# A gated attention and routing block on one core: turning the softmax tile in place, two placed buffers, and a new slot table

## The chip, the cores and the metric

One core of one Trainium2 chip runs the kernel. The metric is device time in microseconds (us). The engines are TensorE (PE, its weight loads PEld), VectorE (DVE), ScalarE (ACT), GpSimd (POOL) and SyncE (SP); SP issues nearly all DMAs here.

## The reference, cut to what matters

```python
# x, ctx: (8, 512, 2048) float32; _layernorm over the last axis (2048)
x = x + tanh(g_xattn) * attn(_layernorm(x), ctx, mask, Wq.. bo)
x = x + tanh(g_ffn)   * route(_layernorm(x), router_weight, router_bias, expert_bias)

def attn(qk, v, ...):        # the 2048 columns are cut into windows of W = 128
    q, k = Wq @ qk + bq, Wk @ qk + bk        # 512 -> 256 rows = 8 heads of 32
    val  = Wv @ v + bv
    scores = einsum('bhdi,bhdj->bhij', qh, kh) / sqrt(32)     # 128 x 128 per head
    scores = where(mask > 0, scores, -1e9)
    o = einsum('bhij,bhdj->bhdi', softmax(scores), vh)
    return (Wo @ gelu(o) + bo) * mask        # 256 -> 512 rows

def route(flat, ...):        # 64 experts, the 8 largest of the softmax are kept
    w = top8(softmax(flat @ router_weight.T + router_bias))
    return flat * w.sum() + w @ expert_bias
```

## The kernel before, in words

A batch is 512 rows by 2048 columns: four tiles of 128 partitions in `X[b % 2]`. The attention works on **units** of 256 columns (two windows): 8 units a batch, 64 in all. float32 products are made of three fp32r passes (`hi*hi`, `lo*hi`, `hi*lo`), so most operands are split in a high part (ScalarE copy) and a low part (GpSimd or VectorE subtraction).

A unit `u` passes through these steps (engine, line of the profile):

- GpSimd z (L1042), ScalarE z_hi (L582), GpSimd z_lo (L1049): the normalised columns. TensorE `project` q and k (L309 to L311, 24 matmuls each), ScalarE q_full, VectorE k_full (L747).
- per window: ctx load (SP L494), ScalarE cx_hi (L598), GpSimd cx_lo (L1055), TensorE v_mm (L324 to L326, 12 matmuls), ScalarE v_full (L604).
- TensorE `scores` (L340: four mask matmuls that open four PSUM banks; L348: 32 tiled 32x128 passes), VectorE `top` (L755, four maxima), ScalarE `expo` (L614, four groups of four exponentials with their sums; L608 brings the table back), VectorE `turn_p` (L762, four transposes of 32x32 blocks), `turn_d` (L767, L771: reciprocals of the sums, spread), SP `move` (L520, 16 DMAs that carry partition quarters of T to PT), TensorE `weigh` (L365, 32 tiled 128x32 passes: the values' products), VectorE `divide` (L777).
- ScalarE `gelu` (L619 table, L622), `o_high` (L631), GpSimd `o_low` (L1066), TensorE `project_out` in two halves WO0 and WO1 (L384 to L386, 12 matmuls each), VectorE `weigh_out` (L790), GpSimd `add_x` (L1061).
- for the router: TensorE `r_turn` (hT, L403, 8 transposes), ScalarE `r_high` (L638), VectorE `r_low` (L820), TensorE `r_mm` (R, L416 and L417), VectorE `stats2` (L803).

Once a batch, after its last unit: ScalarE `c_logits` (L, L644), TensorE `c_turn` (LT, L427), VectorE `c_top` (L841 to L856), ScalarE `c_exp` (L649), VectorE `c_weights` and `c_scale`, TensorE `w_turn` (wT, L438), ScalarE `w_high` (L656), VectorE `w_low` (L883), TensorE `mix` (L453, L454, 16 pairs), ScalarE `scale_x` (L664, four, one per 128 rows), VectorE `add_mix` (x2, L894, 16), SP `store` (L530, 16), then SP `load_x` (L525, 16) of the batch two later into the same buffer, VectorE `input_stats` (bn1, L904, 16) and the norm. The first `input_stats` of each 128 rows waits for all four loads of these rows.

The order of the work on each engine is written out in advance. `SLOTS` gives each step a lag in slots; a unit starts every 16 slots, a batch every 128, a tick is an eighth of a slot. Each engine walks through the ticks and issues what is due: the slots are an order, not times, and no engine waits for a tick. `ENDS` shifts the steps of the last three units. Seven PSUM banks form a ring: `take` gives each product the bank whose planned release is earliest, and the product waits for that release's reader. `PR` is an eighth bank, for R.

In one unit the order on TensorE before is: WO1(u-3), q(u), v, hT(u-3), PV(u-2), k(u), v, WO0(u-2), S(u), R(u-3). `P` is the tile that `expo` writes and `turn_p` reads into `T[u % 2]`; there is one `PT`, so `move(u)` waits for `divide(u-1)`.

## Time and profile before

| | |
|---|---|
| median of 3 runs | 1216.48 us (1215.22 to 2746.26) |
| the profiled execution | 1222.89 us, its span 1221.1 us |
| mean granted TensorE clock | 0.988 |
| TensorE / weight loads busy | 1132.3 / 1046.8 us |
| VectorE / ScalarE / GpSimd busy | 982.0 / 1028.0 / 708.5 us |

The page splits the span by engine, follows back the chain that ended last, and groups instructions by line. A timeline row is start, duration, engine, line, operation, names, count, and in brackets the idle time before it with what ended it. Matmuls overlap, so the cost of one is the distance to the start of the next.

### The profile page before, as it was taken

The page shows a single profiled execution, that of the slowest core. Times are in us where ns is not written, and L with a number is a line of the kernel's source. Part 1 is how long each engine was busy: PE and PEld are TensorE (multiplying, and loading weights), DVE is VectorE, ACT ScalarE, POOL GpSimd, SP SyncE. Part 2 cuts the span into 40 slices and gives each one's busy share as a digit, 9 for nine tenths or more (in the row PEclk, how much of TensorE's full clock was granted, in tenths as well). Part 3 has the DMA queues.
Part 4 walks back from the last instruction along what each step waited for, and adds up shares of the span by engine and source line. Part 5 has one row for each costly group of instructions (what it writes and reads, how often), then busy time and mean ns, then how long its engine had stood idle before and what let it go on. Part 6 is the DMA issues. An engine that isn't in the chain of part 4 may idle for free.

```text
span 1221.1 us, 33356 instructions
## 1 busy us (share of the span) xinstructions
PE 1132.3 (93%) x11661; PEld 1046.8 (86%) x11661; DVE 982.0 (80%) x1921; ACT 1028.0 (84%) x3200; POOL 708.5 (58%) x660
## 2 busy tenths in 40 slices
PE   3799999999999999899999999999999989999976
PEld 3698999899979899788997999988998889979965
DVE  6658879988799877978789887988879877797757
ACT  4698998989988899888998889888998879988944
POOL 2376766467646676466764566646774657655621
PEclk9899999999999999999999999999999989999989
DMA  9377554885548754586546854477544874556433
GB/s 285 82 181 195 137 134 108 249 217 134 126 117 259 209 127 126 176 232 159 131 122 212 218 157 129 110 244 219 135 125 117 265 193 123 130 148 186 109 82 138
DMA packets 169767, 199.82 MB, mean 164 GB/s; under 512 B 27776, under 2 KB 104704, under 8 KB 169472
## 3 DMA queue, kind: packets, MB, share of 16 engines
q1 hardware_dynamic: 168736, 197.69, 59.4%
q8 instruction: 93, 1.52, 0.5%
q14 instruction: 74, 0.61, 0.2%
q10 hardware_dynamic: 864, 0.01, 0.0%
HBM read 80.06 MB, written 33.65 MB: 93 GB/s over the span
## 4 chain that ended last, share of the span: by engine, by line
PE 52%; DVE 15%; SPq 15%; issue 7%; POOL 4%; ACT 4%; DMA 3%; DVEq 0%; POOLq 0%; ACTq 0%
SPq L520 10%; PE ring L309 7%; PE ring L311 6%; PE ring L310 6%; PE ring L365 4%; DVE X L894 3%; PE ring L348 3%; PE ring L324 3%; PE ring L326 3%; PE ring L325 3%; PE ring L384 3%; PE ring L385 3%; PE ring L386 3%; PE ring L403 3%; SPq L525 2%
## 5 line engine op out<-in xcount | busy, mean ns | idle before, releaser
L614 ACT ACTIVATE P<-ring,nmx 128x128 f32<-128x128 f32 x1024 | 358.7, 402 | 55.5 <-DVE nmx L755 55.1
L309 PE MATMUL ring<-z_hi,wqk_hi 128*128 128x256 f32 x1024 | 298.6, 292 | 23.5 <-DVE z_lo L958 21.1
L311 PE MATMUL ring<-z_lo,wqk_hi 128*128 128x256 f32 x1024 | 291.4, 285 | 0.0
L310 PE MATMUL ring<-z_hi,wqk_lo 128*128 128x256 f32 x1024 | 291.3, 285 | 0.0
L614 ACT ACTIVATION_READ_ACCUMULATOR P<-ring,nmx 128x1 f32 x1024 | 248.5, 243 | 0.0
L1049 POOL TENSOR_TENSOR z_lo<-z,z_hi 128x1024 fp32r<-128x1024 f32 x62 | 147.6, 2380 | 164.5 <-ACT z_hi L582 164.5
L309 PEld LDWEIGHTS ring<-z_hi,wqk_hi 128*128 128x128 f32 x1024 | 197.3, 193 | 36.3 <-DVE wqk_lo L933 21.1
L1061 POOL TENSOR_TENSOR X<-X,xt 128x512 f32<-128x512 f32 x128 | 165.2, 1290 | 100.9 <-DVE xt L790 100.5
L762 DVE STREAM_TRANSPOSE T<-P 128x512 f32<-128x512 f32 x256 | 169.1, 690 | 42.5 <-ACT P L614 24.4
L311 PEld LDWEIGHTS ring<-z_lo,wqk_hi 128*128 128x128 f32 x1024 | 197.8, 193 | 0.0
L310 PEld LDWEIGHTS ring<-z_hi,wqk_lo 128*128 128x128 f32 x1024 | 197.7, 193 | 0.0
L1055 POOL TENSOR_TENSOR cx_lo<-cx,cx_hi 128x512 fp32r<-128x512 f32 x128 | 165.9, 1296 | 36.4 <-ACT cx_hi L598 36.4
L755 DVE TENSOR_REDUCE nmx<-ring 128x4 f32<-128x512 f32 x256 | 158.5, 681 | 16.1 <-PE ring L348 15.9
L1066 POOL TENSOR_TENSOR ot_lo<-o,ot_hi 128x512 fp32r<-128x512 f32 x63 | 81.5, 1294 | 148.4 <-ACT ot_hi L631 148.4
L384 PE MATMUL ring<-ot_hi,wo_hi 128*128 128x256 f32 x504 | 143.7, 285 | 12.2 <-POOL ot_lo L1066 12.2
L324 PE MATMUL ring<-wv_hi,cx_hi 128*128 128x256 f32 x512 | 146.6, 286 | 7.8 <-POOL cx_lo L1055 6.0
L790 DVE SCALAR_TENSOR_TENSOR xt<-ring,cst,mg 128x256 f32<-128x256 f32 x256 | 111.3, 476 | 46.1 <-PE ring L386 44.1
L325 PE MATMUL ring<-wv_lo,cx_hi 128*128 128x256 f32 x512 | 145.5, 284 | 0.0
L326 PE MATMUL ring<-wv_hi,cx_lo 128*128 128x256 f32 x512 | 145.4, 284 | 0.0
L386 PE MATMUL ring<-ot_lo,wo_hi 128*128 128x256 f32 x504 | 143.1, 284 | 0.0
L385 PE MATMUL ring<-ot_hi,wo_lo 128*128 128x256 f32 x504 | 142.8, 283 | 0.0
L1042 POOL TENSOR_SCALAR z<-X,ln 128x256 f32<-128x256 f32 x252 | 137.6, 559 | 0.7
(138 smaller groups left out, 2713.3 us busy)
## 6 DMA issues: line engine op xcount, KB each, us to landing
PT<-T SPq DMA_DIRECT2D x1024, 80.0 KB, 2.1
cx<-in_ctx SPq DMA_DIRECT2D x128, 256.0 KB, 3.7
out_y<-X SPq DMA_DIRECT2D x128, 256.0 KB, 3.1
X<-in_x SPq DMA_DIRECT2D x112, 256.0 KB, 4.2
mg<-in_mask SPq DMA_DIRECT2D x64, 128.0 KB, 3.1
X<-in_x SPq DMA_DIRECT2D x8, 512.0 KB, 7.6
sel<-rows_d SPq DMA_DIRECT2D x256, 3.0 KB
X<-in_eb SPq DMA_DIRECT2D x2, 512.0 KB, 8.5
```

The source lines that it names most:

```text
L309: e.matmul(o, wqk_hi[:, t, cols], z_hi[:, t, :], t == 0, False)
L310: e.matmul(o, wqk_lo[:, t, cols], z_hi[:, t, :], False, False)
L311: last = e.matmul(o, wqk_hi[:, t, cols], z_lo[:, t, :], False, t == DT - 1)
L324: e.matmul(o, cx_hi[:, k, :], wv_hi[:, k, :], k == 0, False)
L325: e.matmul(o, cx_hi[:, k, :], wv_lo[:, k, :], False, False)
L326: last = e.matmul(o, cx_lo[:, k, :], wv_hi[:, k, :], False, k == DT - 1)
L384: e.matmul(o, wo_hi[:, m, cols], o_hi[:, m, :], m == 0, False)
L385: e.matmul(o, wo_lo[:, m, cols], o_hi[:, m, :], False, False)
L386: last = e.matmul(o, wo_hi[:, m, cols], o_lo[:, m, :], False, m == 1)
L614: last = e.activation(P[:, n, :], bank("S", 4 * u + g)[:, k * W:(k + 1) * W], ACT.Exp, bias=nmx[u % 2][:, n:n + 1], accum_out=den[u % 2][: ...
L762: e.transpose(T[u % 2][:, :, 4 * g:4 * g + 4, :].rearrange("p b k i -> p k b i"), P[:, 4 * g:4 * g + 4, :].rearrange("p k (b j) -> p k b j ...
L1055: e.tensor_tensor(cx_lo[:], cx[p % NC][:], f32(cx_hi[:]), ALU.subtract).then_inc(cxlo_g, 1)
```

## The change: what it does, and the diff

`P` goes. `expo` writes the exponentials straight into `T[u % 2]`, in the strided layout that the transposes had as output, and `turn_p` transposes each 32x32 block where it stands. `PT` is double, each with its own semaphore. `w2` is laid over `L`. The whole slot table is new. In the new one PV(u) has lag 31.875 and S(u+2) 32, so the values' products stand directly in front of the mask rows and scores of the unit two later. In one unit the order on TensorE becomes: S(u), hT(u-3), q(u+1), WO0(u-2), v, R(u-3), k(u+1), WO1(u-2), v, PV(u-1).

```diff
 SLOTS = dict(
-    rows=-30, z32=-26.25, z_hi=-16, z_lo=-19.75, q=-14, q_ev=-6.25, k=-6.25, k_ev=-6.25,
-    c_hi=-15.5, c_lo=-13.75, v=-10.75, v_ev=-7.5, v_gap=-3.25,
-    S=-1.75, top=1, exp=4, e_gap=0.25, tp=6.25, td=7.25, mv=8.5, PV=25.25, on=23.25,
-    gelu=23, mg=2, ot_hi=24, ot_lo=27.5, WO=27.25, WO_gap=5.75, xt=29.75, x1=31, bn2=39.25,
-    hT=37.5, hT_gap=0.25, ht_hi=41.25, ht_lo=41.75, R=47.25,
-    norm2=27.5, c_base=33.5, L=36, LT=34, c_top=38.75, c_exp=37.75, c_w=40.75, c_sc=40.75, wT=43, wt_hi=43.25, wt_lo=42.25, mix=43.75, m_gap=0.25,
-    sx=44.75, sx_gap=1.25, x2=45.25, rl=48.5, rl_gap=2,
-    x_1=21, x_gap=3.5, bn1=63.25, bn1_gap=2, norm1=101.25,
+    rows=-29, z32=-28, z_hi=-24.25, z_lo=-22.25, q=-14, q_ev=-7.25, k=-6.25, k_ev=-6.5,
+    c_hi=-1, c_lo=2.5, v=6.25, v_ev=7.75, v_gap=-2.25,
+    S=0, top=0.75, exp=4, e_gap=0.25, tp=8, td=9.25, mv=12, PV=31.875, on=29.125,
+    gelu=30.625, mg=13.875, ot_hi=33.375, ot_lo=31.875, WO=36.625, WO_gap=6.75, xt=36.375, x1=39.125, bn2=51.875,
+    hT=48.625, hT_gap=0.5, ht_hi=49.875, ht_lo=49.375, R=55.125,
+    norm2=39.375, c_base=43.625, L=40.875, LT=47.875, c_top=46.875, c_exp=49.625, c_w=49.375, c_sc=49.875, wT=50.375, wt_hi=52.375, wt_lo=51.875, mix=53.375, m_gap=0.25,
+    sx=52.375, sx_gap=0.25, x2=52.375, rl=55.125, rl_gap=1.5,
+    x_1=22, x_gap=4, bn1=67.75, bn1_gap=2, norm1=99.5,
 )
 ENDS = {
...
-        P = sb("P", [128, 16, W])
-        PT = sb("PT", [128, 4, 20, 32])
+        PT = [sb(f"PT{i}", [128, 4, 20, 32]) for i in range(2)]
-        w2 = sb("w2", [128, DT, 2, NX])
+        w2 = L[:].rearrange("p (t a x) -> p t a x", t=DT, a=2)
-        pt_in = sem("pt")
+        pt_in = [sem(f"pt{i}") for i in range(2)]
...                                                     # weigh
-                e.wait_ge(pt_in, 256 * (u + 1))
+                e.wait_ge(pt_in[u % 2], 256 * (u // 2 + 1))
...                                                     # move
-                if u:
-                    e.wait_ge(on_v, u)
+                if u >= 2:
+                    e.wait_ge(on_v, u - 1)
...                                                     # expo
-                if u:
-                    e.wait_ge(tp_v, 4 * (u - 1) + g + 1)
+                if u >= 2:
+                    e.wait_ge(pt_in[u % 2], 256 * (u // 2))
-                    last = e.activation(P[:, n, :], bank("S", 4 * u + g)[:, k * W:(k + 1) * W], ACT.Exp,
-                                        bias=nmx[u % 2][:, n:n + 1], accum_out=den[u % 2][:, n:n + 1])
+                    last = e.activation(T[u % 2][:, :, n, :], bank("S", 4 * u + g)[:, k * W:(k + 1) * W].rearrange("p (b j) -> p b j", b=4),
+                                        ACT.Exp, bias=nmx[u % 2][:, n:n + 1], accum_out=den[u % 2][:, n:n + 1])
...                                                     # c_logits
                 if b:
                     e.wait_ge(lt_pe, b)
+                    e.wait_ge(wT_pe, b)
+                    e.wait_ge(ac_v, b)
...                                                     # turn_p
-                if u >= 2:
-                    e.wait_ge(pt_in, 256 * (u - 1))
                 e.wait_ge(exp_a, 4 * u + g + 1)
-                e.transpose(T[u % 2][:, :, 4 * g:4 * g + 4, :].rearrange("p b k i -> p k b i"),
-                            P[:, 4 * g:4 * g + 4, :].rearrange("p k (b j) -> p k b j", b=4)).then_inc(tp_v, 1)
+                tg = T[u % 2][:, :, 4 * g:4 * g + 4, :].rearrange("p b k i -> p k b i")
+                e.transpose(tg, tg).then_inc(tp_v, 1)
```

`turn_d`, `divide` and `c_weights` change in the same way (`pt_in[u % 2]`, `PT[u % 2]`, `w2`). `ENDS` has new values for all its entries; for the last unit: exp -0.25, tp 2.5, td 3.25, mv 30.25, PV -6.25, on -1.25, gelu 5.75, WO -6, hT 2.25, R 1.5.

## Rows read from the trace of the kernel before

**Rows 1.** The page: busy time by engine, and the last chain by engine.

```profile
PE 1132.3 (93%) x11661; PEld 1046.8 (86%) x11661; DVE 982.0 (80%) x1921; ACT 1028.0 (84%) x3200; POOL 708.5 (58%) x660
PE 52%; DVE 15%; SPq 15%; issue 7%; POOL 4%; ACT 4%; DMA 3%; DVEq 0%; POOLq 0%; ACTq 0%
```

**Rows 2.** Timeline of TensorE, around the tiled products of one unit.

```profile
575.34 1.03 PE L403 MATMUL ring<-ident,X 128*128 128x128 f32 x8
576.30 1.08 PE L365 MATMUL ring<-PT,v 128*32 128x128 f32 x32
577.32 0.39 PE L309 MATMUL ring<-z_hi,wqk_hi 128*128 128x256 f32 x1
577.54 0.28 PE L310 MATMUL ring<-z_hi,wqk_lo 128*128 128x256 f32 x1
...
583.10 0.28 PE L386 MATMUL ring<-ot_lo,wo_hi 128*128 128x256 f32 x1
583.31 0.40 PE L340 MATMUL ring<-sel,ones 32*128 32x512 bf16 x4
...
584.52 0.49 PE L416 MATMUL PR<-ht_hi,wr 128*128 128x512 f32 x1
584.86 0.40 PE L417 MATMUL PR<-ht_lo,wr 128*128 128x512 f32 x1
```

**Rows 3.** Chain of waits: PV of units 5 and 6.

```profile
142.12 1.01 PE ring L365 x32
158.03 1.01 PE ring L365 x32
```

**Rows 4.** Timeline of TensorE: PV of units 0, 3, 32, 33, 34, 61.

```profile
60.51 1.08 PE L365 MATMUL ring<-PT,v 128*32 128x128 f32 x32
...
110.21 1.08 PE L365 MATMUL ring<-PT,v 128*32 128x128 f32 x32 [1.71 <-DMA PT<-T]
...
624.35 1.08 PE L365 MATMUL ring<-PT,v 128*32 128x128 f32 x32
641.68 1.08 PE L365 MATMUL ring<-PT,v 128*32 128x128 f32 x32
669.72 1.08 PE L365 MATMUL ring<-PT,v 128*32 128x128 f32 x32
...
1154.64 1.08 PE L365 MATMUL ring<-PT,v 128*32 128x128 f32 x32
```

**Rows 5.** Waits over the whole span: waiting, for whom, us, times, longest.

```profile
DVE bnst L904 <- DMA X<-in_x: 31.8, 22, 3.9
PE ring L403 <- POOL X L1061: 15.6, 12, 3.6
```

**Rows 6.** Timelines of SP's queue and of VectorE, 977 to 991 us.

```profile
977.75 1.44 SPq L525 DMA_DIRECT2D X<-in_x  x3
...
979.77 11.27 SPq L520 DMA_DIRECT2D PT<-T  x16
...
987.48 0.69 DVE L904 BATCH_NORM_STATS2 bnst<-X 128x6 f32<-128x512 f32 x1 [3.95 <-DMA X<-in_x]
```

**Rows 7.** Timelines in the batch stage: two scalings on ScalarE, eight adds on VectorE.

```profile
652.48 4.12 ACT L664 ACTIVATE X<-X,sc 128x2048 f32<-128x2048 f32 x2
654.73 4.86 DVE L894 TENSOR_TENSOR X<-X,ring 128x512 f32<-128x512 f32 x8
```

**Rows 8.** Groups by line: the exponentials and the transposes.

```profile
L614 ACT ACTIVATE P<-ring,nmx 128x128 f32<-128x128 f32 x1024 | 358.7, 402 | 55.5 <-DVE nmx L755 55.1
L762 DVE STREAM_TRANSPOSE T<-P 128x512 f32<-128x512 f32 x256 | 169.1, 690 | 42.5 <-ACT P L614 24.4
```

**Rows 9.** Timelines at the start and end: move(0), S(63), move(63).

```profile
47.82 11.09 SPq L520 DMA_DIRECT2D PT<-T  x16
...
1161.60 0.39 PE L340 MATMUL ring<-sel,ones 32*128 32x512 bf16 x4
...
1171.91 10.00 SPq L520 DMA_DIRECT2D PT<-T  x16
```

More of the change, by code:

```diff
@@ L364, in weigh @@
                             o = bank("PV", u)[32 * g:32 * g + 32, m * U + w * W:m * U + (w + 1) * W]
-                            last = e.matmul(o, v32[p % NV][:, h * DH:(h + 1) * DH], PT[:, :, 4 * g + 2 * m + w, :], True, True)
+                            last = e.matmul(o, v32[p % NV][:, h * DH:(h + 1) * DH], PT[u % 2][:, :, 4 * g + 2 * m + w, :], True, True)
                 last.then_inc(pv_pe, 1)
@@ L515, in move @@
                 e.wait_ge(td_v, u + 1)
-                if u:
-                    e.wait_ge(on_v, u)
+                if u >= 2:
+                    e.wait_ge(on_v, u - 1)
                 for b in range(4):
                     for a in range(4):
-                        e.dma_start(PT[32 * b:32 * b + 32, a, :, :], T[u % 2][32 * a:32 * a + 32, b, :, :]).then_inc(pt_in, 16)
+                        e.dma_start(PT[u % 2][32 * b:32 * b + 32, a, :, :], T[u % 2][32 * a:32 * a + 32, b, :, :]).then_inc(pt_in[u % 2], 16)
             def load_x(b, t, c):
@@ L769, in turn_d @@
                 if u >= 2:
-                    e.wait_ge(pt_in, 256 * (u - 1))
+                    e.wait_ge(pt_in[u % 2], 256 * (u // 2))
                 e.transpose(T[u % 2][:, :, 16:20, :], rden[:].rearrange("p (b k) -> p b k", b=4).unsqueeze(3).to_broadcast([128, 4, 4, 32])).then_inc(td_v, 1)
@@ L778, in divide @@
                                 bank("PV", u)[:].rearrange("p (k a i) -> p k a i", k=4, a=4),
-                                PT[:, :, 16:20, :].rearrange("p a k i -> p k a i"), ALU.mult).then_inc(on_v, 1)
+                                PT[u % 2][:, :, 16:20, :].rearrange("p a k i -> p k a i"), ALU.mult).then_inc(on_v, 1)
             def weigh_out(u, j):
@@ L865, in c_weights @@
                 e.wait_ge(wm_v, 4 * b + 2)
-                e.tensor_tensor(w2[:], ex[:].unsqueeze(2).to_broadcast([128, DT, 2, NX]),
+                e.tensor_tensor(w2, ex[:].unsqueeze(2).to_broadcast([128, DT, 2, NX]),
                                 sc[:, :, 3:4].unsqueeze(3).to_broadcast([128, DT, 2, NX]), ALU.mult).then_inc(w2_v, 1)
```

10 rows, old and new, of the table ENDS are left out of this document.

## The prediction

> **What bounds the kernel now.** I read the busy times and the last chain, then TensorE's timeline unit by unit, then the waits, then SP's queue behind each batch. TensorE is busy for 93% of the span and VectorE, ScalarE and GpSimd are not far behind; the chain runs over PE for 52%, over DVE and over SP's queue for 15% each [rows 1]. The shares hide that there are three kinds of stage. In an undisturbed unit PE runs without a hole: PV(5) to PV(6) takes 15.91 us [rows 3], against 15.92 us for the issue distances of all its products added up. In the batch stage the period from PV(32) to PV(33) is 17.33 us and to PV(34) 28.04 us [rows 4], 13.5 us over two plain units. Of that about 1.3 us is LT, 0.5 us wT and 16 x 0.47 = 7.5 us mix, so 4.2 us is waiting. Third, from PV(3) at 110.21 to PV(61) at 1154.64 us are 58 periods in 1044.4 us [rows 4]. 58 x 15.92 = 923.4 and 7 x 13.5 = 94.6 leave 26.4 us, and these are holes in the two to four units behind a batch stage. Their cause is in the trace: the statistics of the next batch but one wait on VectorE for the loaded rows, 31.8 us in 22 waits, and PE then waits for GpSimd's X before hT, 15.6 us in 12 [rows 5]. The worst: loads issued until 979.2 us, then 16 moves that fill SP's queue for 11.3 us, and VectorE stands 3.95 us until 987.48 [rows 6], with the next maxima queued right behind.
>
> The sum is made against the profiled execution, 1222.9 us; the median shown is 6.4 us lower (0.5%).
>
> **The tiled products side by side.** Before, PV is followed by q or k at 0.22 us instead of the usual 0.12 (577.32 to 577.54), S starts 0.21 us after the last L386 instead of 0.12, and behind S the first R pass takes 0.34 us instead of 0.23; into PV, behind the transposes, there is no such loss (8 transposes at 0.12 fill 575.34 to 576.30) [rows 2]. So three of four changes between tiled and untiled work cost 0.10 us each, 0.3 us a unit. After, one unit has v to PV, PV to S and S to hT. S to hT costs 0.10 by the same rows. The other two are not in the trace: each lies between 0 and 0.10, so a unit saves between 0 and 0.2 us. I take 0.10, because PV (128x32) and S (32x128) are still two shapes: 64 x 0.10 = 6.4 us, ends 0 and 12.8.
>
> The Trainium skill, TensorEngine Tiling (Array Packing), Key Properties, says that a change of tiling mode drains TensorE, and it speaks against the hope in the new order: PV beside S is still a change of mode. By it alone four changes become three; the sum would be the same 6.4 us if a drain is the 0.10 us of the rows, though the rows show one of the four at nothing.
>
> **P gone, T in place, two PT.** Nothing is added to any engine: the same 1024 exponentials (358.7 us busy, 5.6 us a unit) and 256 transposes of 690 ns [rows 8], the same 16 moves. The transposes already wrote the strided side; now they read it too, and ScalarE writes it in runs of 32. Neither form is in the trace. I cost them at 0. ScalarE is busy 1028.0 / 64 = 16.1 us a unit and VectorE 15.3 [rows 1], batch stages shared out, beside a mean of 1221.1 / 64 = 19.1 us, so a tenth more on the exponentials (0.6 us) is still covered; if the cover went, it would be 64 x 0.6 = 36 us. The waits that go: the exponentials for the transposes of the unit before, and move(u) for divide(u-1). The waits that come: the exponentials and c_logits for a move two units, or a batch, back, long done. move(u) now stands 12 slots behind S(u) and PV(u) 19.9 behind the move (before 16.75), which is what the second buffer pays for. SP needs about 10.5 us for a move, so it can be about 3 us later before PV sees it.
>
> **The slots: plain units.** I wrote out both orders from the tables. Planned distances grow where PE waited: x1 to hT from 0.75 to 2.75 slots, k's product to S from 4.5 to 6.25, z_lo to q from 5.75 to 8.25; a bank for hT has 4 slots of planned slack (before 1.5), for S 7.25 (before 4.5). No plain unit was waiting, so this alone gives 0.
>
> **Behind a batch.** SP's order is as loaded as before: 16 stores, 16 loads, and a move in each unit. Before, the four loads for each 128 rows stand 8.75 slots ahead of the first statistics that need them. After, they are 8.1, 10.1, 12.1 and 14.1 slots ahead, because loads come every 1.5 slots and statistics every 2, and the first statistics of a row come behind the maxima, not in front of them. Walking SP through one batch with 11.27 / 16 = 0.70 us for each DMA of a move (0.63 in the quiet end) and 1.44 / 3 = 0.48 for a load [rows 6, 9], the loads land 1 to 2 us after VectorE asks, at places where VectorE would next wait for PE anyway. So of the 26.4 us I take 15 off; ends 0 and 22.
>
> **The batch stage.** After, S no longer stands among the mix products with its four banks; the mixes all come between S(u) and k. Against that, two of the four exponential groups now stand between the scalings on ScalarE. From the first scaling: three scalings of 2.06 and two groups of 1.4, one copy of ctx of about 0.6, then three adds of 0.61 (the last mix waits for the add of chunk 10) make 11.4 us [rows 7, 8]; before it was 12.3 from the first scaling to the last mix. PE's own work there is 9.9 us. But wT comes sooner behind LT (S, hT and q, 5.1 us, where the logits' chain with its maxima, exponentials and weights takes about 8.6) and waits about 2.5 us longer than its order needs, before 0.8 to 1.3. The two about cancel: 0, ends -14 and +14 (2 us a batch, seven times).
>
> **Start and end.** The first move before is issued from 47.82 to 58.9 us and PV(0) follows at 60.51 [rows 9, 4], behind exponentials that waited for ScalarE's weight copies. The new order brings q(1) and k(1) forward and has only v(0) in front of k(1), so move(0) can go about 2 us sooner; with k(2) also done by then and move(1), move(2) no longer waiting for divisions (PV(3) waits 1.71 us for one now), PV(3) comes about 5 us sooner; ends -8 and +2. At the end S(63) at 1161.60 comes 7.0 us after PV(61) [rows 9, 4], after the change 1 us, with two v and more WO moved behind it into PE's idle time. The move of unit 63 then follows unit 62's on SP, 10.0 us each, so only about 3 us of these 6 arrive: -3, ends -5 and +2.
>
> **Sum:** 6.4 + 15 + 0 + 5 + 3 = 29.4 us; 1222.9 - 29.4 = 1193.5, and with the profiled execution's 0.5% over the median about **1188 us** on the median's scale.
>
> **Rivals.** (A) The sum holds, own range 1172 to 1200: chance 0.50. (B) The holes behind a batch only move. For it: SP's queue is issued almost without pause (15% of the chain [rows 1]), loads still stand behind a move, and the gap of the first four loads is shorter (8.1 against 8.75 slots). Against: what is queued behind the wait is less urgent. The 15 us are lost: 1203; chance 0.20. (C) The adjacency does not do what it says: PV into S costs two changes, and TensorE gains nothing: 6.4 us back, 1194; chance 0.12. (D) More is won than I allow, with the batch stage 2 us shorter too: 1170; chance 0.08. (E) Slower: ScalarE becomes the bound of the batch stage. Its place is the four scalings with the unit's exponentials among them; if they delay the adds for all their 5.6 us, it costs 7 x 5.6 = 39 us, and with it the holes stay as they are: 1216.5 - 14.4 + 39 = 1241. It decides when the add of chunk 10 falls later than PE's own 9.9 us by over 7 us, where I find 1.5. Chance 0.10.
>
> **Numbers.** A measurement of this kernel tells about 2% from no change: under 1192.2 is faster, over 1240.8 slower. A lies about 0.7 of its 0.50 under 1192, D whole, C a little less than half, B hardly: 0.50 faster; E half over 1240.8: 0.06 slower; 0.44 within. The range leaves out part of D and E: 1168 to 1218.
>
> **What would show it.** Adjacency: the period of plain units at 15.82 us (15.72 or 15.92 are the ends). Holes: PV(3) to PV(61) with under 12 us beyond plain units and batch stages, and waits of L904 that no PE wait follows. Batch stage: about 13.3 us over two plain units; 15 or more speaks for E. Start: PV(3) near 105 us; end: the span about 63 us beyond PV(61) (before 66.5). The forecast is wrong if exponentials or transposes grow by over 10%, or if PV waits for PT<-T in plain units.

## The result, and the profile after

The changed kernel takes 1222.57 us (median of 18 runs, 1219.84 to 1226.27), the kernel before on the same chip 1217.94 us (18 runs). The ratio is 1.0038, with a 95% interval from 1.0025 to 1.0051: within 2%, and if anything slower. The forecast was 1188 us, with a range up to 1218. It was wrong. One execution of the kernel before took 2746 us; its median hardly moves with it, and the ratio leaves it out.

| us from the trace | before | after | change | forecast |
|---|---|---|---|---|
| a plain unit | 15.92 | 15.67 | 58 x -0.25 = -14.5 | -0.10 each |
| PV(3) at | 110.21 | 107.59 | -2.6 | -5 |
| 7 batch stages beyond two plain units each | 95.1 | 116.0 | +20.9 | 0 |
| other holes, PV(3) to PV(61) | 26.0 | 22.2 | -3.8 | -15 |
| from PV(61) to the end of the span | 66.5 | 65.3 | -1.1 | -3 |
| span | 1221.1 | 1220.0 | -1.1 | |

A batch stage with the unit ahead of it is two periods, and the plain time of two units is taken off. The prediction had 94.6 and 26.4 us for before, seven times one batch; all seven measured give 95.1 and 26.0. The terms add up to the difference of the two profiled executions. The medians differ by +4.6 us, because the profiled execution of before lay 5 us over the median of its 18 runs and that of after 0.7 us under its own. A part of the 26.0 us of holes may be that execution's own: the new code with the old slots, profiled near its median, has 20.1 us of holes. So the -3.8 us is not shown to be a gain of the change.

The page of the kernel after, busy times and the last chain by engine (they answer to [rows 1]):

```profile
PE 1122.5 (92%) x11661; PEld 1050.9 (86%) x11661; DVE 972.5 (80%) x1921; ACT 1016.8 (83%) x3200; POOL 715.0 (59%) x660
...
PE 54%; DVE 18%; SPq 9%; issue 6%; ACT 5%; DMA 5%; POOL 1%; DVEq 0%; POOLq 0%; ACTq 0%
```

The shares barely move. SP's queue lost 6 points of the chain and GpSimd 3; VectorE gained 3, TensorE and DMA 2 each. TensorE's timeline in one unit of after, and its PV of units 0, 3, 32, 33, 34 and 61 ([rows 2] and [rows 4]):

```profile
707.02 0.28 PE L325 MATMUL ring<-wv_hi,cx_lo 128*128 128x256 f32 x1
707.23 1.08 PE L364 MATMUL ring<-PT,v 128*32 128x128 f32 x32
708.24 0.40 PE L339 MATMUL ring<-sel,ones 32*128 32x512 bf16 x4
708.47 1.06 PE L347 MATMUL ring<-k,q 32*128 32x128 f32 x32
709.46 1.42 PE L402 MATMUL ring<-ident,X 128*128 128x128 f32 x8
...
58.52 1.08 PE L364 MATMUL ring<-PT,v 128*32 128x128 f32 x32 [1.61 <-DMA PT<-T]
107.59 1.08 PE L364 MATMUL ring<-PT,v 128*32 128x128 f32 x32
625.47 1.08 PE L364 MATMUL ring<-PT,v 128*32 128x128 f32 x32
641.13 1.08 PE L364 MATMUL ring<-PT,v 128*32 128x128 f32 x32
673.98 1.08 PE L364 MATMUL ring<-PT,v 128*32 128x128 f32 x32
1154.67 1.08 PE L364 MATMUL ring<-PT,v 128*32 128x128 f32 x32
```

The last v product issues 0.21 us ahead of PV, where 0.12 is usual: a loss of 0.09. PV gives way to the mask rows after the same 1.01 us that 32 products take anywhere, and nothing is lost on either side of it. Behind the scores the first transpose takes 0.17 us instead of 0.11 (627.70 to 627.86 in another unit), a loss of 0.06; q behind the transposes loses nothing that they have not given back (0.85 + 2.96 us for both, 0.97 + 2.87 for the same products before). That is 0.15 us a unit.

Before, it was 0.39, and not the 0.30 of the prediction, which read one change wrongly. Transposes issue 0.11 us apart, and not 0.12, so eight of them in 0.96 us do hold a loss: the last one stands 0.20 us ahead of PV. TensorE before, the last transpose and the first pass of PV:

```profile
576.10 0.27 PE L403 MATMUL ring<-ident,X 128*128 128x128 f32 x1
576.30 0.30 PE L365 MATMUL ring<-PT,v 128*32 128x128 f32 x1
```

So all four changes of before cost 0.09 to 0.11 us, and 0.39 - 0.15 is the 0.25 us of the table within the rounding.

The last rows give 15.66 us from PV(32) to PV(33), so LT no longer lengthens the unit ahead, and then 32.85 us for the batch stage (before 17.33 and 28.04 [rows 4]). Over the seven batches the stage takes 31.66 to 32.85 us, with the unit ahead 47.9 us in the mean, 2.5 more than before; against the shorter plain units that is the 3.0 us a stage of the table. What it waits for stands in TensorE's and VectorE's timelines:

```profile
642.14 1.10 PE L426 MATMUL ring<-id,L 128*128 128x64 f32 x8
652.95 1.09 PE L437 MATMUL ring<-ident,L 128*128 128x128 f32 x4 [4.12 <-DVE L L865]
654.47 0.41 PE L383 MATMUL ring<-ot_hi,wo_hi 128*128 128x256 f32 x1
656.39 0.63 PE L452 MATMUL ring<-eb,wt_hi 128*128 128x512 f32 x1
```

```profile
647.31 1.14 DVE L855 TENSOR_TENSOR lr<-lr,lg 128x256 f32<-128x256 f32 x1
648.37 2.47 DVE L756 TENSOR_REDUCE nmx<-ring 128x4 f32<-128x512 f32 x4
650.76 0.68 DVE L819 TENSOR_TENSOR ht_lo<-ring,ht_hi 128x512 fp32r<-128x512 f32 x1
...
652.11 0.69 DVE L865 TENSOR_TENSOR L<-ex,sc 128x512 f32<-128x512 f32 x1
```

And TensorE's clock in the same stage (the columns: from and to, length, busy us with instructions, granted clock, DMA share, GB/s):

```profile
641.10:653.00 11.90, 7.38 (x110) 0.92 0.47 113
653.00:656.50 3.50, 3.50 (x17) 0.50 0.33 97
656.50:660.00 3.50, 3.08 (x12) 0.78 0.15 56
660.00:674.00 14.00, 13.74 (x91) 1.00 0.87 307
```

In the same place before:

```profile
641.70:653.70 12.00, 9.62 (x93) 1.00 0.41 104
653.70:669.70 16.00, 15.68 (x122) 1.00 0.88 302
```

From the start of LT to wT are 10.8 us, 4.1 of them the wait for the weights and 0.4 a wait of hT for the division. Before, it was 9.7 us, of which only 0.33 were waiting. The three waits of TensorE in that stage before:

```profile
647.59 0.63 PE L438 MATMUL ring<-ident,w 128*128 128x128 f32 x4 [0.33 <-DVE w L866]
649.44 0.36 PE L384 MATMUL ring<-ot_hi,wo_hi 128*128 128x256 f32 x1 [1.23 <-POOL ot_lo L1066]
...
651.93 0.47 PE L453 MATMUL ring<-eb,wt_hi 128*128 128x512 f32 x1 [0.82 <-DVE wt_lo L883]
```

The second and the third are gone in after. So TensorE has 3 us less work between LT and wT, and the chain to the weights is 1.1 us longer. Between the selection (647.31) and the weights' last step (652.11) VectorE now makes the maxima of the scores, which stand at the front of the stage, then ht_lo; before, it was the last turn_p, turn_d and the division, about 2.1 us. Behind the 4.1 us of idling the granted clock is 0.50, the level of 1.2 GHz, for 3.5 us: products of WO issue 0.21 us apart and a pass of a mix takes 0.43. So this wait costs twice. The Trainium skill, TensorE: Matmul & The Clock Gate, "HAM oscillation — how this bites in real kernels", describes this for waits on DMA: the work behind the wait runs at half the clock. This trace agrees, with a wait for VectorE. Over the whole span the waits that answer to [rows 5], and the groups to [rows 8]:

```profile
PE ring L437 <- DVE L L865: 29.5, 8, 4.1
DVE bnst L903 <- DMA X<-in_x: 23.4, 20, 3.2
PE ring L402 <- DVE o L776: 8.2, 11, 2.4
```

```profile
L613 ACT ACTIVATE T<-ring,nmx 128x128 f32<-128x128 f32 x1024 | 362.7, 398 | 1.5 <-DVE nmx L756 1.5
L762 DVE STREAM_TRANSPOSE T<-T 128x512 f32<-128x512 f32 x256 | 168.9, 693 | 53.1 <-ACT T L613 51.9
```

The wait for the weights is there in all batches. The statistics still wait for loads; what follows now is a wait of hT for the division, which is queued behind them (546.77: VectorE waits 3.18 us for X; 548.12: hT waits 2.40 us). That the holes come with the loads is seen behind the seventh stage, where nothing is loaded any more: the three units there take 15.79, 15.67 and 15.67 us, and 15.92 each before. Strided exponentials and in-place transposes cost what the old forms cost.

### The profile page after: what moved, and what is told of

It is laid out like the page before. It is cut to its first block, busy times and chain, and to the rows that moved or that the text cites. A ratio compares the mean times of both kernels' runs of the same rounds, so it can differ in the third digit from the quotient of the medians.

```text
span 1220.0 us, 33112 instructions
## 1 busy us (share of the span) xinstructions
PE 1122.5 (92%) x11661; PEld 1050.9 (86%) x11661; DVE 972.5 (80%) x1921; ACT 1016.8 (83%) x3200; POOL 715.0 (59%) x660
## 4 chain that ended last, share of the span: by engine, by line
PE 54%; DVE 18%; SPq 9%; issue 6%; ACT 5%; DMA 5%; POOL 1%; DVEq 0%; POOLq 0%; ACTq 0%
PE ring L308 6%; SPq L519 6%; PE ring L310 6%; PE ring L309 6%; DMA X<-in_x 5%; PE ring L383 4%; PE ring L384 4%; PE ring L385 4%; PE ring L364 3%; PE ring L323 3%; PE ring L324 3%; PE ring L325 3%; DVE nmx L756 3%; PE ring L347 3%; PE ring L402 3%
## 5 line engine op out<-in xcount | busy, mean ns | idle before, releaser
L613 ACT ACTIVATE T<-ring,nmx 128x128 f32<-128x128 f32 x1024 | 362.7, 398 | 1.5 <-DVE nmx L756 1.5
L613 ACT ACTIVATION_READ_ACCUMULATOR T<-ring,nmx 128x1 f32 x1024 | 244.0, 238 | 0.0
L762 DVE STREAM_TRANSPOSE T<-T 128x512 f32<-128x512 f32 x256 | 168.9, 693 | 53.1 <-ACT T L613 51.9
L383 PE MATMUL ring<-ot_hi,wo_hi 128*128 128x256 f32 x504 | 148.0, 294 | 9.8 <-POOL ot_lo L1065 7.3
L384 PE MATMUL ring<-ot_hi,wo_lo 128*128 128x256 f32 x504 | 146.5, 291 | 0.0
L385 PE MATMUL ring<-ot_lo,wo_hi 128*128 128x256 f32 x504 | 146.2, 290 | 0.0
L1041 POOL TENSOR_SCALAR z<-X,ln 128x256 f32<-128x256 f32 x252 | 140.9, 576 | 4.1 <-DVE z_lo L957 3.4
```

The costliest lines, as they stand in the source:

```text
L383: e.matmul(o, wo_hi[:, m, cols], o_hi[:, m, :], m == 0, False)
L384: e.matmul(o, wo_lo[:, m, cols], o_hi[:, m, :], False, False)
L385: last = e.matmul(o, wo_hi[:, m, cols], o_lo[:, m, :], False, m == 1)
L613: last = e.activation(T[u % 2][:, :, n, :], bank("S", 4 * u + g)[:, k * W:(k + 1) * W].rearrange("p (b j) -> p b j", b=4), ACT.Exp, bias=n ...
L762: e.transpose(tg, tg).then_inc(tp_v, 1)
```

## The experiments

All ratios are to the kernel before, run beside each, with the 95% interval in brackets. A single stage is the period from the batch stage's PV to the next; a total for the stages is that of the table, seven of them with the unit ahead, beyond two plain units each. The totals of after, e6, e7 and e10, whose waits in the stage are alike, are 116.0, 113.4, 115.2 and 114.7 us, so a difference of 1 or 2 us between totals says nothing. The labels in brackets, e1 to e17, are used further down. Edits are to the changed kernel if nothing else is said.

### The two halves of the change

**Code alone (e2).** The new code with the slots of before.

```diff
-SLOTS, ENDS of the changed kernel
+SLOTS, ENDS of the kernel before
```

> The changed kernel's code (T turned in place, P gone, two PT) with the slot tables of the kernel before. Theory 1 (the buffers by themselves give and cost nothing, everything measured comes from the order): 1.000 of the kernel before within 0.3%, exponentials at 402 ns and transposes at 690 ns within 2%, plain unit 15.92 us. Rival 1 (the strided writes or the in-place transposes are slower and eat the gain): exponentials over 410 ns or transposes over 705 ns, and 3 to 10 us slower than before. Rival 2 (the single PT held moves up): 3 us or more faster than before, with fewer waits of PV for PT<-T.

1215.63 us, 0.9959 [0.9934, 0.9984]. Plain units 15.92, stages as before (94.7 us in all), holes 20.1. PV(61) comes at 1148.60, 6.0 us sooner than in the profile before, which lay 5 us over its median. The exponentials take 402 ns and the transposes 690. So the buffers and the transposes in place cost nothing and bring about 5 us (2 to 8 by the interval), nearer to rival 2 than to theory 1; but not by its mechanism, since PV's waits for PT<-T did not get fewer (7.4 us, before 5.9). Turn_p's waits for the move, 16.9 us in 28 before, are gone; whether this is the gain stays open. This is the fastest kernel of the study.

**Slots alone (e3).** The old code with the new slots.

```diff
-SLOTS, ENDS of the kernel before
+SLOTS, ENDS of the changed kernel
```

> The kernel before (P, one PT) with the changed kernel's slot tables. Theory 1 (the new order has PV so late that move(u) has to wait for divide(u-1), which needs the second PT): each move starts only after PV(u-1), 10.5 us of issue and 2.1 us of landing fill 12.6 + 1.7 = 14.3 of the 15.67 us of a unit, so plain units may just hold, but behind batch stages moves cannot catch up: 10 to 40 us slower than the changed kernel. Rival (the second PT buys nothing on this core): within 5 us of the changed kernel.

1243.2 us, 1.0199 [1.0152, 1.0246]. Plain units 15.67, the stages 115.6 us (after 116.0), other holes 39.6 (after 22.2). All of the plain units' gain and all of the stages' loss come from the order; the second PT and T are worth 17.4 us of holes in it.

### The adjacency

**PV apart from S (e1)**, with v between them.

```diff
-PV=31.875
+PV=27.875
```

> The changed kernel with PV's lag at 27.875 instead of 31.875: PV then stands between WO1 and v, no longer against S. Theory 1 (the adjacency is what shortened the plain unit from 15.92 to 15.67 us): the plain unit goes back to about 15.9 us and the time rises by 64 x 0.25 = 16 us, to about 1.013 of the changed kernel. Rival (the 0.25 us come from S standing before the transposes of hT and R standing between v and k, not from PV against S): the plain unit stays under 15.75 us and the time within 5 us of the changed kernel's.

1247.39 us, 1.0223 [1.0181, 1.0264]. The plain unit takes 16.27 us, 0.60 more. Of these 0.20 are the two changes that are paid again (the first v product's neighbour comes 0.23 us behind it, not 0.12, and the mask rows 0.21 us behind v); most of the rest is a new wait of WO for ot_lo. Read from the issue distances, PV beside S is worth 0.20 of the 0.25 us a unit. The time cannot show it alone.

```profile
699.11 1.08 PE L364 MATMUL ring<-PT,v 128*32 128x128 f32 x32
700.12 0.39 PE L323 MATMUL ring<-wv_hi,cx_hi 128*128 128x256 f32 x1
700.35 0.28 PE L324 MATMUL ring<-wv_lo,cx_hi 128*128 128x256 f32 x1
...
701.54 0.28 PE L325 MATMUL ring<-wv_hi,cx_lo 128*128 128x256 f32 x1
701.75 0.40 PE L339 MATMUL ring<-sel,ones 32*128 32x512 bf16 x4
```

**hT away from S (e8)**, behind q.

```diff
-hT=48.625, ... ht_hi=49.875, ht_lo=49.375
+hT=50.125, ... ht_hi=50.375, ht_lo=50.25
```

> The changed kernel with hT behind q (lag 50.125; its copies shifted with it), so that S is followed by q and no longer by the transposes. My forecast had S to hT cost 0.10 us; the trace shows 0.85 + 2.96 us for hT and q, about their bare work. Theory 4 (transposes behind a tiled product hide the change, any other product pays 0.10 us): the plain unit rises from 15.67 to about 15.77 us, 6 us in all. Rival (it is PV against S alone that saves the changes, what stands behind is indifferent): 15.67 us.

1315.33 us, 1.077 [1.0725, 1.0816]. The plain unit takes 17.07: q behind S takes 2.98 us instead of 2.87, so scores into q cost 0.11 us, where scores into transposes cost 0.06; hT standing there is worth the other 0.05 of the 0.25 us. So theory 4 is right that q pays and wrong that transposes hide the change. The other 1.3 us of the unit are a new wait, of WO behind hT for a bank that ht_lo frees (74.9 us in 59 waits), so this time says nothing of the adjacency.

### The holes behind a batch

**Whole rows (e6)**: x is loaded in one DMA for each 128 rows instead of four.

```diff
-                e.dma_start(X[b % 2][:, t, c * 512:(c + 1) * 512],
-                            xv[b, t, :, c * 512:(c + 1) * 512]).then_inc(x_in[b % 2][t], 16)
+                if c == 0: e.dma_start(X[b % 2][:, t, :], xv[b, t]).then_inc(x_in[b % 2][t], 16)
```

> The changed kernel with each 128 rows of x loaded by one DMA of 2048 columns where the first of its four quarter loads stood (the others go). SP then has 4 load issues a batch and not 16, and they stand earlier. Theory 3 (the holes behind a batch, 22.2 us in all, come from loads issued late in SP's queue, behind moves): the holes fall to under 10 us and the kernel is 10 to 15 us faster than the changed one; waits of the statistics for X under 8 us (before 23.4). Rival (what is late is the transfer itself, 1 MB beside moves and ctx loads): holes within 4 us of 22 us.

1222.28 us, 1.002 [0.9994, 1.0047]; holes 21.0 (after 22.2). They moved: PV now waits for the move, 2.52 us at 554.42, and a load takes 7.3 us to land instead of 4.8. So how often SP issues is not what makes the holes, which speaks for the rival, the transfer itself. That the moves and the loads slow each other down is not shown by any run.

### What holds the batch stage

**The scalings (e7)**: left out for three quarters of the columns in batches 0 to 6.

```diff
-... else (slice(0, S),)
+... else (slice(0, S if b == NB - 1 else 512),)
```

> The changed kernel with the scaling of x (ScalarE) done on 512 of the 2048 columns in batches 0 to 6; the other three quarters are left unscaled, so this part of the computation is left out. It takes 4 x 1.4 us off ScalarE in each batch stage. Theory 2 (scalings and adds bind the stage): the stage is 3.5 to 5.5 us shorter, 25 to 38 us in all. Rival 1 (the wait for wT and the planned banks bind it): under 1.5 us a stage, under 10 us in all. In both cases wT still waits 4.3 us.

1220.12 us, 1.001 [0.9984, 1.0036]; stages 115.2 us, the wait for the weights 4.1. The scalings do not bind in this order, and the mechanism of the prediction's rival E falls.

**wT and the mixes late (e4)**, at one go in front of k.

```diff
-wT=50.375, ... mix=53.375, m_gap=0.25
+wT=54.5, ... mix=55.75, m_gap=0.125
```

> The changed kernel with wT (lag 54.5) behind WO0 and v, and mix (lag 55.75, gap 0.125) behind both R, so that TensorE has 1.44 + 1.43 us more to do while VectorE and ScalarE work out the weights. Theory 1 (the gain of the plain units is lost in the batch stage because wT stands 4.3 us too early in TensorE's order): the wait before wT falls from 4.3 us to under 1.5, the batch stage is 2 to 3.5 us shorter and the kernel 14 to 25 us faster than the changed one. Rival (the batch stage is bound by ScalarE's scalings between the exponentials and VectorE's adds, and the wait for wT only covers that): the wait moves to the last mix products, the stage keeps its 32.1 us within 1 us and the time stays within 6 us.

1234.72 us, 1.0116 [1.0069, 1.0163]. wT waits no more, but 16 mixes in a row take 0.68 us each, near the 0.62 us of one add, and wait for adds: stages 128.7 us. The first half of theory 1 held, its gain did not come.

**The scalings behind the exponentials (e5).**

```diff
-e_gap=0.25, wt_hi=52.375, sx=52.375, sx_gap=0.25, mix=53.375, wt_lo=51.875
+e_gap=0.125, wt_hi=52.125, sx=52.5, sx_gap=0, mix=54.375, wt_lo=52.25
```

> The changed kernel with another order in the batch stage: on ScalarE the four exponential groups and wt_hi first, then the four scalings in a row (e_gap 0.125, wt_hi 52.125, sx 52.5 with gap 0, wt_lo 52.25 as a planned time), and mix one slot later (54.375), behind v. The trace of the changed kernel has the first scaling end at 656.6 and the last at 667.3 us, 10.7 us for 8.2 us of scaling, with two exponential groups and a 1.2 us wait for v between them. Theory 2 (the batch stage is bound by the scalings, the adds that wait for them and the banks that wait for the adds): the scalings end after 8.3 us from their start, the stage falls from 32.1 to about 29.5 us and the kernel is 12 to 25 us faster than the changed one. Rival (the stage is set by when wT is ready): the stage keeps 32.1 us within 0.7 us.

1233.59 us, 1.0105 [1.0067, 1.0143]. Stages 112.3 us, 3.7 less, but the unit behind takes 17.59 and the holes 33.5. The wait for the weights stays 4.1, as the rival had it.

**The order on VectorE and ScalarE alone (e10)**: exponentials of the router earlier, with their table loaded in advance, weights in front of the maxima.

```diff
-c_exp=49.625, c_w=49.375
+c_exp=46.875, c_w=48.625
...
+                e.activation(tab[:, 2:3], half[:, 0:1], ACT.Exp)   # c_exp, ahead of its wait
```

> The changed kernel with the router's exponentials and weights issued earlier on ScalarE and VectorE as in e9, but wT still in its ring bank, which the second ht_lo frees, and wt_hi where it was. Theory: two things end at nearly the same moment, the weights (652.8) and the bank's release; with the maxima now behind the weights both ht_lo come no earlier (about 653), so the wait for wT stays about 4 us and the time about 1220 (within 2 us). Rival (the weights alone are the wait, the bank does not matter): wT's wait falls to about 1 us and the time to 1206 to 1213 as in e9.

1222.76 us, 1.0032 [1.0006, 1.0059]. wT starts no earlier, as expected: it waits 4.1 us for ht_lo, which frees its bank. Stages 114.7 us.

**The same, and wT in the router's own bank (e9)**, wt_hi in front of the attention exponentials.

```diff
+c_exp=46.875, c_w=48.625, wt_hi=51.875, and c_exp's table as above
-... e.transpose(bank("wT", b)[:, ...]   # w_high and w_low read bank("wT", b)
+... e.transpose(PR[:, ...]             # w_high and w_low read PR
+                    e.wait_ge(wtlo_v, b)        # r_mm, first of a batch
```

> The changed kernel with the way to the expert weights shortened. ScalarE loads the exponential table while it waits and issues the router's exponentials before ctx and o are split; VectorE makes the weights in front of the maxima of the scores instead of behind them and behind ht_lo; the weights' transposes write the router's own accumulator bank, which is free by then, instead of a ring bank that ht_lo frees; wt_hi is issued in front of the attention exponentials. Theory (the batch stage grew because the new order makes TensorE reach wT while this chain on VectorE and ScalarE is not done): in the trace of the changed kernel the weights were ready at 652.8 and the selection they need at 648.45, so wT starts about 3 us earlier, its wait falls from 4.3 to about 1 us, the batch stage falls from 32.3 to about 30, and 7 of them give 10 to 17 us: 1206 to 1213. Rival 1 (what binds is the banks and adds of the 16 mixes, as when they were put in a row): the wait moves to the mixes, stage 32, time 1220. Rival 2 (the maxima, 1.2 us later, hold the attention exponentials, so the next unit is late): stage shorter but the unit behind it 17 us, time 1218.

1222.04 us, 1.0026 [1.0001, 1.0051]; stages 114.8 us. TensorE's timeline:

```profile
648.92 0.66 PE L433 MATMUL PR<-ident,L 128*128 128x128 f32 x4 [1.14 <-DVE L L862]
651.91 0.39 PE L381 MATMUL ring<-ot_hi,wo_hi 128*128 128x256 f32 x1 [2.34 <-DVE ht_lo L816]
```

wT comes 8.8 us behind PV instead of 11.8, and WO takes over the wait, for a bank that the second ht_lo frees. The clock then falls as in after, to 0.57 for 3.5 us, behind two waits of 1.1 and 2.3 us. The first mix starts 14.2 us behind PV (after 15.3), and nothing of it reaches the time: rival 1 and its 1220 us.

**Clock held (e11)**: wT in the router's bank, and 16 needless products in front of its wait.

```diff
+                keep_on(PR[:], 20 if b == NB - 1 else 16)   # w_turn
```

> The changed kernel; in each batch stage TensorE runs 16 needless products of 512 columns (about 3.8 us at 0.24 us each, as the mixes' issue spacing) into the router's bank just before it waits for the weights, and the weights' transposes write that bank too. Nothing else is moved, so the weights are ready as late as in the changed kernel. The trace of the changed kernel shows a granted clock of 0.50 for the 3.5 us behind the 4.1 us wait and 0.78 for the next 3.5 us; at full clock that work is about 2.5 us shorter. Theory (the wait costs twice, once as idle time and once as clock behind it): the granted clock of the stage stays near 1.00 and the 12 products of WO start 0.12 us apart, not 0.21; the stage falls from 32.3 to about 30 and 7 of them give 10 to 17 us: 1206 to 1213. Rival (VectorE's adds and the banks set the stage, the slow products are hidden behind them): clock 1.00, WO 1.4 us, but the mixes wait the difference; stage 32, time 1219 to 1222.

1217.88 us, 0.9988 [0.9969, 1.0006]; stages 109.0 us, each 31.1 to 31.3. The clock of the stage:

```profile
638.20:650.20 12.00, 11.23 (x127) 1.00 0.47 113
650.20:653.70 3.50, 3.30 (x22) 1.00 0.31 94
653.70:657.20 3.50, 3.17 (x20) 1.00 0.64 239
657.20:669.40 12.20, 11.67 (x77) 1.00 0.84 299
```

The weights are as late as ever. With the clock held a stage is 0.8 us (against e10) to 1.0 us (against after) shorter, and the time 0.5% against the changed kernel (0.9988 to 1.0038). The 2.4 us that the slow products had cost TensorE do not all come back, because the mixes then wait 0.3 to 0.9 us for adds, 0.3 to 0.5 for exponentials and 0.2 for wt_lo; the forecast was 1.2 us a stage too hopeful, and the truth lies between it and the rival. wT's move to the router's bank came with this edit, and no run has it alone.

**Weights, then both ht_lo, then the maxima (e12)**, on the kernel of e9, with 6 needless products.

```diff
                 for b in batch(t, C["c_w"]):
                     c_weights(b)
+                    for a in range(2): r_low(NU * (b + 1), a)   # b < NB - 1; ahead of top(u)
```

> The kernel of e9 with two more steps: VectorE makes both ht_lo of the stage's unit directly behind the weights, in front of the maxima of the scores (they free the bank that WO waited 2.3 us for in e9), and TensorE runs 6 needless products of 512 columns (1.4 us) before it waits for the weights. Theory (every wait of the stage that e9 left is on VectorE's order, and each costs clock too): wT at 8.8 us behind PV as in e9, WO directly behind it, clock near 1.00 (e9: 0.57 for 3.5 us), so the stage falls from 32.3 to about 29 and 7 of them give about 20 us: 1196 to 1206. Rival 1 (the wait moves on to wt_lo or the adds of the mixes): stage 31 to 32, time 1215 to 1222. Rival 2 (the maxima come 2.5 us later than in the changed kernel and the next unit's attention with them): stage 29 but a longer unit behind it, time 1210.

1232.02 us, 1.0099 [1.0078, 1.012]; stages 124.1 us. WO starts directly, and the first mix waits 2.58 us for wt_lo, which stands behind the maxima now:

```profile
657.78 0.36 PE L381 MATMUL ring<-ot_hi,wo_hi 128*128 128x256 f32 x1 [0.54 <-POOL ot_lo L1067]
662.04 0.47 PE L449 MATMUL ring<-eb,wt_hi 128*128 128x512 f32 x1 [2.58 <-DVE wt_lo L880]
```

**Scores behind the mixes**, in the batch stages only. First on the kernel of e9 (e13), then on the changed kernel (e14).

```diff
+for u in range(11, 60, 8):
+    for n, later in (("S", 6.875), ("top", 5), ("exp", 2.875), ("tp", 4.5), ("td", 4.25), ("mv", 2.5)):
+        ENDS[n, 64 - u] = later
-v_ev=7.75
+v_ev=6.75
```

> The kernel of e9 (weights early) with 6 needless products in front of the wait for the weights, and in the batch stages alone the scores of the unit two later, their maxima, exponentials, transposes and moves are put behind the first 6 mixes, as the kernel before has them behind 10; v's eviction is a slot earlier on ScalarE in all units. The plain units keep the new order and their 15.67 us. Theory (the stage is longer because scores, 2.5 us of maxima and 5 us of exponentials stand in front of the weights and the mixes' banks): the stage falls from 32.3 to 28 to 29.5, 7 of them give 20 to 30 us, holes as before: 1190 to 1202, the fastest kernel so far. Rival 1 (VectorE's 28 us of work is the bound in any order): stage 31 to 32, 1215 to 1222. Rival 2 (the late move of the stage's unit makes its PV late two units on): stage 29, but the units behind it together 2 to 3 us longer: 1210.

> The changed kernel with only the scores' group of the batch stages put behind the first 6 mixes (and v's eviction a slot earlier), the weights' chain, its bank and the order on ScalarE as in the changed kernel, and no needless products. Theory: the maxima (2.47 us) no longer stand in front of the weights on VectorE, so wT starts about 2 us earlier although 1.7 us of scores are gone from in front of it; stage 29 to 31, time 1200 to 1212, 3 to 12 us over e13. Rival (VectorE's total): 1220.

1277.83 us, 1.0492 [1.047, 1.0514], and 1294.26 us, 1.0625 [1.0593, 1.0656]. The theory is refuted as built: stages of 36.6 to 39.8 us and of 39.6 to 41.9. From the first to the last mix are 18.4 to 20.9 us (after 10.6 to 11.5), with the score banks, the maxima and the exponentials among them. A better set of places may exist. What e14 tells of the chain to the weights is on VectorE and TensorE:

```profile
680.84 0.69 DVE L823 TENSOR_TENSOR ht_lo<-ring,ht_hi 128x512 fp32r<-128x512 f32 x1 [1.70 <-ACT ht_hi L641]
683.25 1.09 PE L441 MATMUL ring<-ident,L 128*128 128x128 f32 x4 [5.26 <-DVE L L869]
```

The maxima are gone from in front of the weights, and LT to wT is still 10.4 us. VectorE now stands and waits for ht_hi, which comes behind gelu, the table's load and the router's exponentials on ScalarE, and the weights stand behind ht_lo. So the maxima alone account for 0.4 us of the 10.8; only with the router's exponentials earlier, the weights ahead of both and a bank of its own does wT come 3 us sooner (e9).

**The adds (e15)**: three quarters of each left out in batches 0 to 6.

```diff
-                e.tensor_tensor(xs, xs, bank("mix", i)[:], ALU.add)
+                n = 512 if b == NB - 1 else 128
+                e.tensor_tensor(xs[:, 0:n], xs[:, 0:n], bank("mix", i)[:, 0:n], ALU.add)
```

> The changed kernel, but in batches 0 to 6 VectorE adds only the first 128 of each 512 columns of the experts' part (the result of those batches is left incomplete); all instructions, their order and their waits stay. It takes about 0.4 of 0.62 us off each of 16 adds, 6 to 7 us of VectorE's 28 in a stage. Theory (order): the wait for the weights (4.1 us) and the slow clock behind it stay, and only what waits for banks behind mix 4 is gained: stage 31 to 32, time 1213 to 1220. Rival (VectorE's total work is the bound): the stage falls by 3 us or more, to about 29, and the time to 1200 or less.

1219.17 us, 1.0007 [0.999, 1.0024]; stages 112.1 us, 0.6 less each, the wait for the weights unchanged. Some 6 us of VectorE's work a stage gone for at most 0.6 us: its total work is not the bound. That leaves the order, on VectorE and ScalarE, in front of wT.

**LT early (e16)**, in front of the second half of WO of the unit ahead, with the router's steps behind it; wT in the router's bank.

```diff
-c_base=43.625, LT=47.875, c_top=46.875, c_exp=49.625, c_w=49.375, wt_hi=52.375
+c_base=41.625, LT=43, c_top=43.25, c_exp=45.25, c_w=45.25, wt_hi=51.875
```

> The changed kernel with LT, 5 slots earlier, between k and the second half of WO of the unit ahead (about 3 us in front of PV), and the router's base, logits, maxima and selection on VectorE, its exponentials on ScalarE (in front of gelu, where the exponential table is still loaded) and its weights on VectorE moved forward with it, the weights directly behind the division of o. wT writes the router's bank, wt_hi stands in front of the attention exponentials; wT, the mixes, the scores and all else keep their places. Theory (the stage is longer because LT to wT has 5.5 us of products for a chain of 8.6 to 10.8 us, and idle time and slow clock follow): LT to wT has 9 to 10 us of products now, the weights are ready before wT, no wait at wT, granted clock near 1.00; the stage and the unit ahead together fall from 48.0 to about 43 to 45 (LT keeps its 1 us), 7 times 3 to 5 us give 20 to 35: 1187 to 1202. Rival 1 (the maxima and the two ht_lo hold WO's bank, then the adds hold the mixes): 1 to 1.5 us a stage: 1212. Rival 2 (VectorE's router work in the unit ahead delays the division and gelu of the unit, so that WO waits for ot): stage and unit ahead 47 to 48: 1218 to 1222.

1257.18 us, 1.032 [1.0294, 1.0346]. Two rows of TensorE:

```profile
655.64 1.08 PE L425 MATMUL ring<-id,L 128*128 128x64 f32 x8 [2.73 <-ACT L L641]
...
675.45 0.80 PE L448 MATMUL ring<-eb,wt_hi 128*128 128x512 f32 x1 [3.37 <-DVE X L889]
```

and one of VectorE:

```profile
674.71 1.29 DVE L889 TENSOR_TENSOR X<-X,ring 128x512 f32<-128x512 f32 x2 [3.90 <-ACT X L661]
```

The first half of the theory holds: wT waits no more. But LT waits for L, and the first mixes are reached 5 to 6 us earlier, only to wait for an add that waits for a scaling that stands behind eight attention exponentials. The stage is still 31.0 to 31.8 us, and the unit ahead 19.5 to 22.6.

**Both of these cured (e17)**: LT behind v, the first scaling in front of the exponentials.

```diff
-LT=43, ... c_exp=45.25, ... sx=52.375, sx_gap=0.25      # of e16
+LT=44.25, ... c_exp=45.625, ... sx=51.875, sx_gap=0.5
```

> The kernel of e16 with LT behind v instead of in front of WO (1.4 + 1.5 us of products later, when L is there), the router's exponentials behind v's eviction on ScalarE, and the first scaling in front of the attention exponentials, the others among them. Theory (in e16 the wait for L, 2.7 us, and the wait for the first scaling, 3.9 us, ate the gain): the unit ahead falls back from 21 to about 17 us, the stage from 31.7 to 28.5 to 30, together 45 to 47 (changed kernel 47.9, e16 52.8): 1196 to 1214. Rival (the stage is one serial chain over VectorE and ScalarE from L to the adds, some 21 us of VectorE work in it, and each cut shows the next wait: the maxima and ht_lo in front of WO's bank): together 48 to 49, 1218 to 1228.

1245.1 us, 1.0213 [1.018, 1.0245]. The unit ahead is 16.6 us, as expected, the stage 33.6 to 34.5. hT now waits for the division, which stands behind the logits, and the mixes wait for exponentials (26.5 us in 12 waits, up to 3.7), which hold the banks and stand behind the scaling. Together 50 to 51 us, over the 48 to 49 of the rival.

## Why the prediction was wrong

**The failed step** is "The two about cancel: 0" for the batch stage. It cost 20.9 us. The forecast had seen the piece that mattered, wT closer behind LT, priced its wait at 2.5 us beyond the order's need, and set against it a gain between the first scaling and the last mix. Three things were wrong in it:

- The wait. It is 4.12 us, before 0.33, so 3.8 more. From the end of LT the chain to wT takes 9.8 us and not 8.6, which is about what it took in the old order (8.7): on VectorE the maxima (2.47 us) and ht_lo (0.68) slid in between selection and weights, and on ScalarE ht_hi and the table's load stand in the way (e14). A walk over the two queues of the new order would have shown it.
- The gain. From the first scaling to the last mix the forecast had 11.4 us for 12.3. Measured are 12.1 to 13.3 us, before 12.5 to 12.6, and 12.0 to 12.1 with the clock held (e11): next to nothing. Leaving out three quarters of the scalings did not shorten the stage either (e7).
- The clock, which the sum did not have at all: 0.8 to 1.0 us a stage (e11).

The sign that the prediction gave for rival E came true, 16.6 us over two plain units where 15 or more was to speak for it. Its mechanism did not (e7), so the sign was a bad one.

**What holds the stage** is shown as far as this: it is the order, not the code (e3 against e2), not the scalings' work (e7), nor VectorE's total (e15). Of the 3.0 us a stage that it grew, 3.8 are the wait for the weights and 0.8 to 1.0 the clock, and 2.1 come off because the waits for ot_lo and wt_lo of before are gone; 0.3 to 0.5 are not accounted for. Removing the wait for the weights leaves a wait at WO (e9), at wt_lo (e12), at the adds behind a scaling (e16), or at the exponentials' banks (e17). VectorE and ScalarE serve two chains at once, the router's and the scores', and with the scores in front of the stage both want the same 10 us. The kernel before has the scores behind 10 mixes. That this is the cause is argued from these waits and not shown: the attempts to put the scores back (e13, e14) were slower still. It stays open.

**The adjacency** was right in mechanism and too small: 0.25 us a unit, over its upper end of 0.20. The upper end was too low because the change from the transposes into PV was taken for free; it cost 0.09 like the others. Four losses before, 0.39 us in all; two after, 0.09 into PV and 0.06 behind the scores. PV beside S costs nothing that can be read (forecast: 0.10 between the two shapes), and S into hT 0.06 (forecast: 0.10). The Trainium skill, TensorEngine Tiling (Array Packing), Key Properties, has each change of mode drain TensorE. The trace agrees for every change between 128x128 and tiled products; between PV's 128x32 and the scores' 32x128 it shows no cost, and there the trace decides. Rival C falls.

**The holes** gave 3.8 us at most and not 15, and against e2's 20.1 us nothing. The second PT and T carry this order (without them 39.6 us, e3), but VectorE still waits for loads (23.4 us, before 31.8), and fewer and earlier issues do not help (e6). This was rival B. The sum missed by 28.3 us between the two profiles: 20.9 in the stages, 11.2 in the holes and 4.3 at the two ends, less 8.1 that the plain units gave beyond the forecast. That the time lies only 5 us outside the range is in part luck: without the plain units' 8.1 us it would be 13.

**Start and end**: -2.6 for -5, and -1.1 for -3. PV(0) comes 2.0 us sooner, with the move ahead of it; the other 3 us that the forecast gave PV(3) did not come. At the end S(63) comes right behind PV(61), its mask rows after 1.0 us as forecast, but its move comes only 12.4 us later. TensorE, VectorE, then SP's queue:

```profile
1155.91 1.06 PE L347 MATMUL ring<-k,q 32*128 32x128 f32 x32
```

```profile
1167.55 0.71 DVE L770 STREAM_TRANSPOSE T<-rden 128x512 f32<-128x512 f32 x1
```

```profile
1153.19 11.28 SPq L519 DMA_DIRECT2D PT<-T  x16
1168.33 10.02 SPq L519 DMA_DIRECT2D PT<-T  x16
```

SP is done with unit 62's move at 1164.5 and with two mask loads at 1167.1; unit 63's starts at 1168.33, as turn_d ends (1168.26). So it is not SP's queue that holds it, as the forecast had it, but the maxima, exponentials and transposes in front. It is issued 3.6 us sooner (before 1171.91 [rows 9]), and 1.1 us of them arrive: PV(63) waited 1.35 us for its move before, now it does not and comes at 1182.30 instead of 1183.42.

**Buffers and transposes at 0**: right (398 and 693 ns; before 402 and 690).

## What to carry to other kernels

A new order for the frequent unit must be walked through the rare stage too, on every queue between a wait's source and its reader: here 0.25 us won 58 times was lost to 3 us seven times. Cost an idle stretch of TensorE like these 4 us twice, once as time and once as the slow clock behind it; where it can't be removed, products into a free bank win some of the second cost back, here 0.8 to 1.0 of 2.4 us. Measure the spacing of each kind of product before calling a change between them free. And when a wait is taken away, ask first which wait is due a microsecond later, because a stage that is built of two interleaved chains pays out only when all of them move.

## What the runs showed of the hardware that was not expected

- Every change of the plain units between products of 128x128 (transposes too) and tiled products costs TensorE 0.06 to 0.11 us (before, after, e1, e8); PV's form (128x32) directly in front of the mask rows and scores (32x128) costs nothing that can be read.
- After 4.1 us of waiting the granted clock was 0.50 for 3.5 us and 0.78 for the next 3.5; with needless products in place of the wait it was 1.00 throughout (e11). Two waits of 1.1 and 2.3 us, 0.7 us of work apart, brought it to 0.57 (e9); the waits of 0.3, 1.2 and 0.8 us in the same place before left it at 1.00.
- One load of 2048 columns landed in 7.3 us (median), where the loads of 512 took 4.8 us each, beside the same moves (e6).
